# Attention stage of a graph layer: queries held as three 16-bit parts, their selectors made by VectorE

## The reference, cut to what matters

```python
h = jnp.maximum(_layernorm(x, axis=-1), 0.0)
Q, K, V = h @ Wq, h @ Wk, h @ Wv                      # (n, 8, 32) each
score = jnp.einsum('ehd,ehd->eh', Q[dst], K[src]) / np.sqrt(32)
score = score + jax.nn.relu(efeat @ W1 + b1) @ W2 + b2
ex = jnp.exp(score - jax.ops.segment_max(score, dst)[dst])
alpha = ex / jax.ops.segment_sum(ex, dst)[dst]
out = jax.ops.segment_sum(alpha[:, :, None] * V[src], dst)
x = x + out.reshape(n, 256) @ Wo + bo
```

## Time and profile before

| | us |
|---|---|
| median of three timed runs | 5838.89 (5834.64 to 5838.99) |
| the profiled execution | 5842.13 |
| its span in the trace | 5840.2 |
| `edge_tables` (to about 111 us, with the first loads) | 111 |
| `node_projections` (about 111 to 262 us) | 150 |
| `attend` (about 262 to 2870 us) | 2608 |
| of it with the edge network and all sums (340 to 2700 us) | 2360 |
| of it after the edge network has ended (2700 to 2870 us) | 170 |
| second layer (to the end) | 2970 |

### The profile page before, as it was taken

How to read it: one execution, slowest core, us unless ns; L and a number is a source line. 1 busy time by engine, 2 the same in 40 slices (tenths; PEclk the granted TensorE clock), 3 DMA queues, 4 the chain that set the end, 5 groups by cost and what they waited for, 6 DMA issues and landing times. The chain is left out here.

```text
span 5840.2 us, 108440 instructions
## 1 busy us (share of the span) xinstructions
PE 5074.5 (87%) x22962; PEld 3057.4 (52%) x22963; DVE 3406.7 (58%) x7903; ACT 3349.0 (57%) x8126; POOL 3313.4 (57%) x3407
## 2 busy tenths in 40 slices
PE   5899999999999999999699999776777777777775
PEld 3566666666666666666444444344444444444443
DVE  3289999999999999999733333332333233333323
ACT  1488888888888888887544444333333333333332
POOL 1166666666666666666400000477777777777775
PEclk8999999999999999999899999766566566665665
DMA  2477777777777777777544444433333333333334
GB/s 84 146 215 222 222 221 223 220 224 223 222 221 221 222 223 223 221 222 218 163 133 142 141 141 141 119 105 104 104 104 105 103 104 105 104 104 105 105 103 125
DMA packets 634844, 942.30 MB, mean 161 GB/s; under 512 B 166045, under 2 KB 468255, under 8 KB 634783
## 3 DMA queue, kind: packets, MB, share of 16 engines
q0 software_dynamic: 212992, 661.34, 39.3%
q1 hardware_dynamic: 421790, 280.26, 16.5%
HBM read 808.29 MB, written 132.98 MB: 161 GB/s over the span
## 5 line engine op out<-in xcount | busy, mean ns | idle before, releaser
L911 POOL DMA_INDIRECT kv_rows<-kv_d,idx x1664 | 1667.5, 1002 | 930.3 <-issue 463.3
L1352 PE MATMUL m_sums<-m_rows,m_oh 128*128 128x256 f32 x3328 | 1537.1, 611 | 579.1 <-issue 205.0
L1314 POOL DMA_INDIRECT m_rows<-msg_d,m_idx x1664 | 1594.3, 958 | 537.1 <-issue 377.7
L1352 PEld LDWEIGHTS m_sums<-m_rows,m_oh 128*128 128x128 f32 x3328 | 897.0, 297 | 1219.4 <-issue 687.8
L1664 ACT ACTIVATE m_rows<-m_rows,m_norm 128x256 f32<-128x256 f32 x1664 | 754.2, 500 | 1360.7 <-DMA m_rows<-msg_d,m_idx 1360.7
L1374 DVE TENSOR_TENSOR agg<-agg,m_sums 128x256 f32 x832 | 350.5, 421 | 1452.3 <-PE m_sums L1352 1452.1
L1088 PE MATMUL sums<-kv_rows,onehot 128*128 128x264 f32 x3328 | 932.6, 403 | 10.6 <-DVE kv_rows L1213 3.6
L1049 PE MATMUL p_q<-q,pickT 128*128 x3328 | 868.7, 384 | 13.4 <-ACT pickT L954 9.0
L1088 PEld LDWEIGHTS sums<-kv_rows,onehot 128*128 128x128 f32 x3328 | 573.2, 190 | 385.6 <-issue 313.3
L1635 PE MATMUL p_m<-wr,h1T 128*128 128x512 f32 x1568 | 710.5, 596 | 0.0
L931 ACT ACTIVATE hid<-p_hid,b1s 128x512 f32<-128x512 f32 x784 | 496.3, 684 | 370.5 <-PE p_hid L1027 370.5
(11 more groups left out here) (180 smaller groups left out, 4455.9 us busy)
## 6 DMA issues: line engine op xcount, KB each, us to landing
msg_d<-msg SPq DMA_DIRECT2D x196, 512.0 KB
dsts<-dstrow_d SPq DMA_DIRECT2D x416, 128.0 KB
ef_raw<-in_edge_attr_dram SPq DMA_DIRECT2D x195, 256.0 KB
kv_rows<-kv_d,idx POOLq DMA_INDIRECT x1664
m_rows<-msg_d,m_idx POOLq DMA_INDIRECT x1664, 2.8
kv_d<-kvo SPq DMA_DIRECT2D x49, 260.0 KB
pens<-pens_d SPq DMA_DIRECT2D x104, 96.2 KB
emlp<-mlp_d SPq DMA_DIRECT2D x104, 64.0 KB
```

The costliest lines, as they stand in the source:

```text
L911: pool.indirect_dma_start(rows[:, u, k, :], None, kv_d[:, :], bass.IndirectOffsetOnAxis(idx[:, half, c:c + 1], 0)).then_inc(gathered[u], 16)
L1314: pool.indirect_dma_start(rows[:, u, k, :], None, table[:, :], bass.IndirectOffsetOnAxis(idx[:, u // 2, c:c + 1], 0)).then_inc(gathered[u] ...
L1352: last = nc.tensor.matmul(sums[u % BANKS][:, 0:width], onehot[:, u % HOTS, k, :], rows[:, u, k, :], start=(k == 0), stop=(k == 1))
```

## The change

1. `q` and `att` become views of one tensor, `shelf`, of 50 rows of 768 16-bit numbers a partition. Queries of block b lie in row b + 1 as three bf16 parts of 256; the sums of block b lie, as f32, in row b. Since the sums can't be cleared beforehand, `add` multiplies the old value by `keep[s]`, 0 in a block's first step and 1 else: an operation with two inputs and a scalar read from SBUF in place of an addition. `keep` is made in `edge_tables` by two operations of DVE. POOL clears only row 0.
2. `node_projections` splits: ACT writes the scaled query rounded to bf16 (same operation and line of work); DVE then does `split` (exact rest from PSUM, in f32), `second` (rest rounded to bf16) and `third` (what is left). `second` and `third` run one and two blocks behind. PE also waits for `split` before it uses a PSUM slot again. `split` of block j stands ahead of DVE's other work of step j.
3. `select` issues six bf16 matmuls, three parts for each of the two halves, accumulated in PSUM.
4. ACT's `measure` and `pick` go. DVE's new `pick(s + 3)`, one comparison of bf16 with a per-partition scalar, bf16 out, stands between the two operations of `dot(s)`. DVE now waits for the load of `dsts` and, in place of ACT, for `q_done`.

```diff
+            shelf = att_ctx.enter_context(nc.sbuf_tensor("shelf", [P, BLOCKS + 1, 3 * D], BF16, side="right"))
+            q = shelf[:, 1:BLOCKS + 1, :]
+            att = shelf[:, 0:BLOCKS, :].bitcast(F32)[:, :, 0:H * HD1]
...
+            nc.vector.memset(t["keep"][:, 0:1], 0.0)
+            nc.vector.tensor_tensor(t["keep"][:, 1:TSTEPS], nbase[:, 1:TSTEPS], nbase[:, 0:TSTEPS - 1], ALU.is_equal)
...
+            def split(i, j):
+                n = B * i + j
+                dve.wait_ge(q0_ready, n + 1)
+                nc.vector.scalar_tensor_tensor(out=qr[:, j, :], in0=qq[SLOT[j]][:, 0:D], scalar=HD ** -0.5, in1=q_part(0, n),
+                                               op0=ALU.mult, op1=ALU.subtract).then_inc(qr_ready, 1)
+                if not (first and j < 1):
+                    second(n - 1, (j - 1) % B)
+                if not (first and j < 2):
+                    third(n - 2, (j - 2) % B)
...
             def iteration(i, more):
                 for j in range(B):
+                    split(i, j)
                     if more:
...
-        pickT = sb("pickT", [P, PICKS, 2 * P])
+        pickT = sb("pickT", [P, PICKS, 2 * P], BF16)
...
-                    last = nc.tensor.matmul(p_q[u % 2][:, k * D:(k + 1) * D], pickT[:, u % PICKS, k * P:(k + 1) * P],
-                                            q[:, bass.ds(b, 1), :], start=True, stop=True)
+                    for part in range(3):
+                        last = nc.tensor.matmul(p_q[u % 2][:, k * D:(k + 1) * D], pickT[:, u % PICKS, k * P:(k + 1) * P],
+                                                q[:, bass.ds(b, 1), part * D:(part + 1) * D].rearrange("p b d -> p (b d)"),
+                                                start=(part == 0), stop=(part == 2))
...
+                nc.vector.tensor_scalar(pickT[:, u, :], dsts[:, u, :], t["node"][:, 0:1], None, ALU.is_equal).then_inc(pick_ready, 1)
...
+                if is_step(s + 3):
+                    pick(s + 3, (u + 3) % U, U * n + (u + 3) // U)
                 dve.wait_ge(prod_done, s + 1)
...
-                nc.vector.tensor_tensor(to, to, sums[u % 2][:, 0:KV - D].unsqueeze(1), ALU.add).then_inc(added, 1)
+                nc.vector.scalar_tensor_tensor(out=to, in0=to, scalar=t["keep"][:, bass.ds(s, 1)], in1=sums[u % 2][:, 0:KV - D],
+                                               op0=ALU.mult, op1=ALU.add).then_inc(added, 1)
```

More of the change, by code:

```diff
@@ L533, in _ @@
             pool.memset(kvo[:, :, D:KV], 1.0).then_inc(ones_set, 1)
-            pool.memset(att[:, :, :, :], 0.0)
+            pool.memset(att[:, 0, :], 0.0)
         @block.vector
@@ L593, in _ @@
             iteration(BATCHES - 2, True)
+            iteration(BATCHES - 1, False)
+            second(BLOCKS - 1, B - 1)
+            third(BLOCKS - 2, B - 2)
+            third(BLOCKS - 1, B - 1)
         @block.scalar
@@ L1002, in body @@
                         weights(c, (u // R - 1) % 2)
-            for s in range(3):
-                measure(s, s, 0)
-                pick(s, s)
             act.wait_ge(w_in, WIN)
@@ L1132, in _, with pick @@
         def _(dve):
+            def pick(s, u, n):
+                if u % 2 == 0:
+                    dve.wait_ge(dsts_in[u // 2], 16 * (n + 1))
+                if not (isinstance(s, int) and s < PICKS):
+                    dve.wait_ge(q_done, s + 1 - PICKS)
+                nc.vector.tensor_scalar(pickT[:, u, :], dsts[:, u, :], t["node"][:, 0:1], None, ALU.is_equal).then_inc(pick_ready, 1)
             def dot(s, u, n, x):
@@ L1257, in _ @@
             dve.wait_ge(cleared, 2 + H)
+            for s in range(3):
+                pick(s, s, 0)
             passes(dve, body)
```

50 lines of the change are left out of this document (22 added, 28 removed).

## The result

| | before | after |
|---|---|---|
| median of 12 timed runs each, side by side | 5835.74 (5833.25 to 5838.99) | 5848.14 (5843.50 to 5853.28) |
| ratio, 95% interval | | 1.0019 [1.0011, 1.0027] |
| the profiled execution | 5842.13 | 5847.10 |

What follows compares the result with a forecast made beforehand. TensorE was taken as the bound, by only 1.5 us in a chunk of 25, VectorE close behind. Fused stage -24, tail +7, projections +14, tables +1 sum to -2 us: median 5837 us, range 5795 to 5882.

Steps and rivals of the forecast that it cites:

- the comparison: Fused stage, VectorE's new `pick`: takes 0.19 us, adds 0.08 us a step, since it stands in the gap before the reduction.
- the pointer: Fused stage, VectorE's addition: reading `keep` as a scalar from SBUF costs 0.06 us a step.
- the tail's chunk: Chunk after the edge network has ended, VectorE's own period: from 23.40 to 24.52 us.
- the tail +7: Last 52 steps, 6.5 chunks without edge network, VectorE's already: 1.12 us more each, 7 us lost.
- TensorE's saving: Fused stage, selection: six bf16 matmuls instead of four f32 records save 0.18 us a step, between 0.12 and 0.21.
- comparison by numbers: Rival, fused stage: `pick` runs at the rate of numbers, not bytes, 0.15 us a step; 5880 us; chance 0.15.
- hindrance from POOL: Rival, fused stage: gathers block `pick`, some 0.3 us a step; near 6070 us; chance 0.03.
- cheaper scalars: Rival, fused stage: scalars from SBUF hold VectorE no longer, both new terms lose 0.06 us; 5796 us; chance 0.18.
- What is left of the wait for TensorE: Fused stage, light steps: VectorE's wait falls from 1.52 to 0.15 us a chunk, chunk 24.67 against 24.92; 24 us gained.
- Projections: Node projections: `split` ahead of the next batch's normalisation makes TensorE wait at six batch changes; 14 us lost.
- the stand: Projections: TensorE stands still for 2.4 us at each of the six batch changes.

Runs made afterwards that it cites:

- e6: Changed kernel with the constant 0.0 instead of the pointer to `keep` as the addition's scalar, leaving the running sums out; 5813.7 us, ratio to before 0.9965.
- e3b: Changed kernel with the selectors made by ScalarE in two operations again, bf16 result, three parts and `keep` kept; 5822.68 us, ratio to before 0.9979.
- e4c: Changed kernel with TensorE's turn of `drop`'s results issued one step later, on a fast chip; 5880.06 us, ratio to before 1.0077.
- e4: Changed kernel with TensorE's turn of `drop`'s results issued later, on a chip where every kernel is slower; 6712.60 us, ratio to before there 1.0152.

## Why the prediction was wrong

*Prices.* TensorE 0.75 us a step (forecast 0.74 to 0.65, saving 0.21 at the upper end), the comparison 0.19 and its net 0.08, the pointer 0.06 to 0.07, the tail's chunk 24.51 (24.52), the tail +7: right. TensorE's saving was taken as 0.18, which alone would have made the forecast too cautious. The rivals fell with them: no comparison by numbers (281 ns, not 335), no hindrance from POOL (a mean of 281 ns, 15 above L1171's in the earlier trace rows, beside gathers that take 67% of the time, and the next operation starts at most 0.21 us after it, in all 708 cases between 400 and 2600 us), cheaper scalars neither. The contention that the Trainium skill names ("GPSIMD Engine Reference", Specifications) is not seen here for gathers.

*What is left of the wait for TensorE: the step that failed in the fused stage.* It subtracted four savings of TensorE and four new costs of VectorE in the light steps from a wait of 1.52, which left 0.24, and lowered that to 0.15 for a TensorE "further ahead". The wait that was left is 24.86 - 24.51 = 0.35. Two things were wrong. TensorE can't be further ahead than the product of step 3, which VectorE makes after its heavy steps and for which the selection of step 5 waits. And so what VectorE takes longer in the heavy steps isn't hidden: it holds TensorE back by as much. The rows of the kernel before, VectorE and TensorE, had this handover already:

```profile
1503.67 0.43 DVE L1231 TENSOR_TENSOR att<-att,sums 128x264 f32 x1 [0.55 <-PE sums L1088]
...
1517.75 0.67 DVE L1138 TENSOR_TENSOR prod<-p_q,kv_rows 128x512 f32<-128x512 f32 x1
...
1528.59 0.43 DVE L1231 TENSOR_TENSOR att<-att,sums 128x264 f32 x1 [0.55 <-PE sums L1088]
```

```profile
1518.69 1.11 PE L1049 MATMUL p_q<-q,pickT 128*128 x4
```

The product ends at 1518.42 and the selection begins 0.27 us later; over the chunks between 600 and 2600 us that distance is 0.25 to 0.31, in about every other chunk 0.25, and in the others TensorE has no gap in front of the selection. So before the change TensorE's own work and the loop were the same length within 0.06 us, and the loop read from these rows is the whole chunk: 14.75 + 0.27 + 9.90 = 24.92. A busy share of 2357 in 2360 us doesn't show that. The change made TensorE's part 0.65 shorter, three of a chunk's eight selections (3 x 0.21), and VectorE's part 0.50 longer in the mean and 0.57 between the two chunks shown (five additions at 0.06 and four comparisons at 0.04 to 0.08 would be 0.58). In the means 25.00 - 0.65 + 0.50 + 0.01 = 24.86. That the loop is the cause, three experiments show, each of which moved one part alone (e6, e3b and e4c in the table above).

The chunk came out 0.19 above the forecast's 24.67, 18 us over the stretch, but the gain missed by 11 only: the forecast subtracted from one chunk of 24.92, while the mean was 25.00. Those 7 us are luck. TensorE's saving of 0.21 instead of 0.18 helped too.

*Projections: the term that was too small.* The order was right, the stand was right (2.25 for 2.4 us), and the sum lacked the clock that falls behind most such stands: 14 us were forecast, and 4 or 6 spells of 1.7 us, 7 to 10 us, came on top. The prediction had argued from the tail before, with TensorE busy 85% at 1.00, that a somewhat idler TensorE keeps its clock. That row holds for its stretch and no further: in the tail after the change TensorE is busy 80% (136.43 of 170 us), and the clock has spells at 0.50 there too, a mean of 0.94. They cost nothing that shows, as VectorE sets the pace of the tail.

*The whole.* -13 + 7 + 20 + 1 - 1 + 1 = +15, against -2 forecast. The time lies well within the range, on its slower side, but for two reasons that none of the rivals named; that the range held is no merit of the reasoning.

## What to carry to other kernels

Price a change of the second-busiest engine by the loop that would bind next: follow the handovers from one engine to the other and back, and count only the instructions that lie on each side of it; here five of eight additions and three of eight selections. A busy share of 99.9% doesn't say whether the engine also waits for another one: look at the distance from the release to the start, and whether it is always the same. Where a new operation stands ahead of work that another engine waits for, first try the order: moving two calls gave back 23 us here. Before moving an instruction out of an engine's wait, look at what the next one would wait for, and what the moved one then delays, as at the turn of e4. And a cost of 2 us in which TensorE stands still has to be priced with the clock that may follow it.

## What was unexpected about the hardware

A stand of 2.03 to 2.25 us at full load, once in 22 to 24 us, was followed by some 3.4 us at 0.50 in 10 of 12 cases (two profiles of the same kernel), worth 1.7 us each; five useless matmuls in its place left no such spell and made the projections 8 to 12 us shorter. With one part of three, TensorE, busy 82% of a fast chunk, dropped to 0.50 in 44 of 95 chunks, and the kernel with less work was 61 us slower than the one with more. Chips differ: the same kernel took 5832 to 5836 us on some and 6609 to 6614 on two others, which made 16% fewer gathers in the same time. A single execution can begin 18 us late.
